# Moving a routed part ahead of the dense one, halving bursts of indirect DMAs and merging a gate product in a fused token-mixing, state-space and mixture-of-experts layer

## The reference

```
h  = prelu((dgamma * (q k^T)) v Wo + bo)        # q, k, v = x Wq + bq, ...; no softmax
n  = layernorm(h)
A  = exp(-softplus(n Wd + bd));  u = (1 - A) * (n WB + bB) * (n Wx + bx)
s_t = A_t * s_(t-1) + u_t                        # scan over 1024 tokens
h  = h + ((n WC + bC) * s) Wy + by
n  = layernorm(h)
top 2 of 16 experts of softmax(n gate_w + gate_b), their weights made to sum to 1
h  = h + sum over the 2 experts of weight * (silu(n w1) * (n w2)) w3
```

## Time and profile before

| | |
|---|---|
| median of 3 timed runs | 258.33 us (256.31 to 261.71) |
| span of the profiled execution | 331.5 us; no time of its own is given beside the span |
| mean granted TensorE clock in it | 0.846 of full speed |
| TensorE busy | 257.1 us, 78% of the span |
| VectorE, ScalarE, GpSimd busy | 160.1, 119.7, 98.2 us |

### The profile page before, as it was taken

How to read it: one execution, slowest core, us unless ns; L and a number is a source line. 1 busy time by engine, 2 the same in 40 slices (tenths; PEclk the granted TensorE clock), 3 DMA queues, 4 the chain that set the end, 5 groups by cost and what they waited for, 6 DMA issues and landing times.

```text
span 331.5 us, 4678 instructions
## 1 busy us (share of the span) xinstructions
PE 257.1 (78%) x1645; PEld 156.7 (47%) x1645; DVE 160.1 (48%) x283; ACT 119.7 (36%) x283; POOL 98.2 (30%) x119
## 2 busy tenths in 40 slices
PE   8999999988935976258829995169964899952995
PEld 7443332532411323136529884168642698621563
DVE  1453649789805993167705610053410466710664
ACT  1302561764108711467534541022320344311341
POOL 4000000004760077303771047600476000674000
PEclk9999999999985999658965997555796599995699
DMA  7999800000111101332221675995121323021101
GB/s 191 371 388 278 170 0 0 4 0 12 40 51 57 33 20 52 89 95 73 55 58 44 154 160 131 209 222 114 41 59 28 83 65 78 19 44 20 34 16 32
DMA packets 45990, 29.74 MB, mean 90 GB/s; under 512 B 32688, under 2 KB 41072, under 8 KB 45456
## 3 DMA queue, kind: packets, MB, share of 16 engines
q1 hardware_dynamic: 30416, 23.15, 27.1%
q10 hardware_dynamic: 12480, 3.15, 4.3%
q0 software_dynamic: 3072, 3.15, 3.9%
HBM read 20.46 MB, written 8.98 MB: 89 GB/s over the span
## 4 chain that ended last, share of the span: by engine, by line
PE 52%; another core or an unknown queue 19%; ACT 11%; DVE 10%; issue 7%; ACTq 0%; POOL 0%; DVEq 0%; POOLq 0%
PE ring L1013 10%; PE ring L971 9%; PE turn L988 7%; PE side L1025 5%; PE acc L816 4%; PE ring L802 4%; ACT squares L611 3%; PE side L843 3%; DVE mixed L1141 2%; PE ring L759 2%; PE side L775 2%; ACT n L629 2%; PE acc L934 1%; DVE state L1190 1%
## 5 line engine op out<-in xcount | busy, mean ns | idle before, releaser
L559 POOL DMA_INDIRECT slots<-n,slot_i x48 | 47.8, 996 | 121.9 <-DVE slot_i L1256 108.2
L1283 DVE TENSOR_TENSOR act<-ring,silu 128x512 f32<-128x512 f32 x56 | 38.4, 690 | 89.5 <-ACT silu L681 68.6
L569 POOL DMA_INDIRECT back_v<-results,slot_i x48 | 46.5, 968 | 81.4 <-DMA results<-res 67.7
L681 ACT ACTIVATE silu<-ring 128x512 f32<-128x512 f32 x56 | 33.3, 597 | 78.7 <-remote 38.5
L1141 DVE TENSOR_TENSOR mixed<-ring,dg 128x1024 f32<-128x1024 f32 x32 | 38.6, 1218 | 19.5 <-remote 10.9
L816 PE MATMUL acc<-mixed,v 128*64 128x512 f32 x128 | 34.3, 628 | 8.6 <-DVE mixed L1141 8.4
L802 PE MATMUL ring<-kq 64*128 64x512 f32 x128 | 33.5, 629 | 0.0
L1013 PE MATMUL ring<-nT,w_sb 64*128 64x256 f32 x128 | 24.2, 459 | 8.8 <-issue 8.0
L971 PE MATMUL ring<-slots_t,w_shared 64*128 64x128 f32 x192 | 19.8, 328 | 13.7 <-issue 12.7
L988 PE MATMUL turn<-w_sb,act 128*128 128x64 f32 (+1 forms) x192 | 29.1, 314 | 0.0
L988 PEld LDWEIGHTS turn<-w_sb,act 128*128 128x128 f32 x192 | 27.3, 226 | 3.0 <-issue 2.2
(11 more groups left out here) (150 smaller groups left out, 306.5 us busy)
## 6 DMA issues: line engine op xcount, KB each, us to landing
dg<-dgT SPq DMA_DIRECT2D x8, 512.0 KB, 7.8
dg<-given SPq DMA_DIRECT2D x8, 512.0 KB, 15.7
slots<-zeros SPq DMA_DIRECT2D x3, 1024.0 KB, 13.2
w_shared<-w SPq DMA_DIRECT2D x48, 64.0 KB, 2.2
slots<-slots SPq DMA_DIRECT2D x12, 256.0 KB
results<-res ACTq DMA_DIRECT2D x12, 256.0 KB, 2.9
w_sb<-w SPq DMA_DIRECT2D x2, 1024.0 KB, 14.3
xs<-xT SPq DMA_DIRECT2D x4, 256.0 KB, 6.5
```

Of the source, the lines that this page charges most:

```text
L559: pool.indirect_dma_start(out=slots_dram[r], out_offset=bass.IndirectOffsetOnAxis(ap=slot_i[:, r, k, i:i + 1], axis=0), in_=n2[:, u % 2, i ...
L569: pool.indirect_dma_start(out=back_v[:, r, i, k, :], out_offset=None, in_=results_dram[r], in_offset=bass.IndirectOffsetOnAxis(ap=slot_i[: ...
L681: s.activation(silu[:, n % 2], hidden_banks(n)[:, :, 0:PAIRS * P], ACT.Silu).then_inc(silu_done, 1)
L1283: dve.tensor_tensor(act[:, n % ACT_BUFS], hidden_banks(n)[:, :, PAIRS * P:2 * PAIRS * P], silu[:, n % 2], ALU.mult).then_inc(act_done, 1)
```

## The change

In words, in the order of the diff:

- `take_raw` now copies rows and raw gate products together (160 columns a tile); `center2` makes both in one matmul per half tile set, from the joined matrix `cg`. The logits are then read from SBUF.
- In each beat `place`, `spread` and `give_slots` come last on VectorE, and their beats are later for units 0 and 1 (slots 25 to 28) with `spread` ahead of `slots`. On ScalarE `scale_rows` comes after `relus`, `norm_squares` and `norm_std` of the next unit.
- Eight indirect DMAs are waited for before the other eight of a part are issued, in scatter and gather.
- All 32 dense groups come after r2. The spread of the dispatch matrix is cut into 8 loads instead of 4, and placed after slot loads 10 and 11; `weigh` begins at pair 10, two pairs ahead of use. Combines come earlier, result buffers are 4 instead of 2.
- The first pair of routed groups is issued at beats 62 to 68; the first turned slots go through the bank `ring`.
- At the start 30 warm-up matmuls stand instead of 70, two loads are issued from ScalarE's queue, and V1, K1, Q1 of the first half are projected at beat 2.
- The fifth set of shared weights is loaded after the fourth slot load instead of ahead of the first.

```diff
-    "center2": (16, 17), "turn_h": (21, 17), "count": (24, 21), "owner_row": (27, 14), "prelu": (0, 0),
+    "center2": (16, 17), "turn_h": (20, 19), "count": (24, 24), "owner_row": (31, 27), "prelu": (0, 0),
-    "logits": (19, 18), "mark0": (19, 19), "one0": (22, 19), "mark1": (22, 20), "one1": (22, 21), "place": (25, 24),
-    "slots": (25, 24), "spread": (25, 27), "owners": (30, 35), "weights": (24, 22), "dispatch": (4, 22),
+    "logits": (19, 18), "mark0": (19, 19), "one0": (22, 19), "mark1": (22, 20), "one1": (22, 21), "place": (27, 25),
+    "slots": (28, 25), "spread": (27, 25), "owners": (33, 30), "weights": (24, 22), "dispatch": (4, 22),
...
-WEIGHTS_AFTER = (-2, -2, -2, -2, -1, 3, 3, 6, 7, 7, 9, 11)
-
-GIVEN_AFTER = 9
-SPREAD_AFTER = 9
+WEIGHTS_AFTER = (-2, -2, -2, -2, 3, 3, 3, 6, 7, 7, 8, 8)
+
+GIVEN_AFTER = 10
+SPREAD_AFTER = {10: (0, 1), 11: (2, 3, 4, 5, 6, 7)}
+FIRST_WEIGH = 10
...
-FFN_BEAT = 65
-
-FFN_RATES = (1, 2, 1, 2, 1, 1, 0, 1, 0, 1, 1, 1, 2, 0, 1, 1, 1, 1, 2, 4, 0, 3, 0, 1)
+FFN_BEAT = 62
+
+FFN_RATES = (4, 1, 0, 0, 3, 1, 1, 0, 0, 0, 0, 0, 0, 1, 1, 2, 0, 1, 1, 1, 1, 2, 4, 0, 3, 0, 1)
-RES_BUFS = 2
-GIVEN_LOADS = 4
+RES_BUFS = 4
+GIVEN_LOADS = 8
-DENSE_RUNS = (0, 0, 8, 24)
+DENSE_RUNS = (0, 0, 0, 32)
-COMBINE_AFTER = (13, 14, 20, 22, 24, 27)
-WARM = 50
-WARM2 = 20
+COMBINE_AFTER = (11, 13, 16, 18, 22, 25)
+WARM = 30
...
                 for i in range(UT):
+                    if i == UT // 2:
+                        pool.wait_ge(scattered[r], 16 * UT)
                     for k in range(2):
...
-                s.activation(n2[:, u % 2].rearrange("p i d -> p (i d)"), side[:, 1, :], ACT.Copy).then_inc(raw_taken, 1)
+                s.activation(n2[:, u % 2].rearrange("p (k t) c -> p k t c", k=2), cg_tiles(), ACT.Copy).then_inc(raw_taken, 1)
...
-                    mm = pe.matmul(side[:, 1, t * P:(t + 1) * P], hT[:, u % 2, t * P:(t + 1) * P], center_m[:, :],
+                    mm = pe.matmul(side[:, t // 2, t % 2 * CG:(t % 2 + 1) * CG], hT[:, u % 2, t * P:(t + 1) * P], cg[:, :],
                                    start=True, stop=True)
                 mm.then_inc(cen_done[1], 1)
-                for t in range(TT):
-                    mm = pe.matmul(side[:, 0, t * 2 * NE:(t + 1) * 2 * NE], hT[:, u % 2, t * P:(t + 1) * P], gate_w[:, :],
-                                   start=True, stop=True)
-                mm.then_inc(raw_done, 1)
```

More of the change, by code:

```diff
@@ L67 @@
 VW, VB, VO, VCOLS = 0, 128, 256, 320
+CG = P + 2 * NE
 BEAT = {
@@ L143, in due @@
     units = ROUTED_UNITS if name in ROUTING else (DENSE_UNIT,) if name in DENSE_WORK else range(UNITS)
-    return [u for u in units if m - unit_end(u) == BEAT[name][u == LAST]]
+    last = ROUTED_UNITS[-1] if name in ROUTING else LAST
+    return [u for u in units if m - unit_end(u) == BEAT[name][u == last]]
 def scores_at(m):
@@ L378, in turned_sum, with cg_tiles @@
             return side[:, 1, 0:GB * D]
+        def cg_tiles():
+            return side[:, :, 0:2 * CG].rearrange("p k (t c) -> p k t c", c=CG)
         def count_bank(u):
@@ L495, in _ @@
                     store_given()
-                if n == SPREAD_AFTER:
-                    for i in range(GIVEN_LOADS):
-                        spread_given(i)
+                for i in SPREAD_AFTER.get(n, ()):
+                    spread_given(i)
                 for k in range(len(SHARED_NO)):
@@ L567, in gather @@
                 for i in range(UT):
+                    if i == UT // 2:
+                        pool.wait_ge(gathered[r * COMBINES], 16 * UT)
                     for k in range(2):
@@ L605, in norm_squares @@
                     s.wait_ge(raw_taken, u + 1)
-                rows_ = (turn[:, :], n2[:, u % 2].rearrange("p i d -> p (i d)"))[which]
                 if u == LAST:
-                    s.activation(squares[:, :, :].rearrange("p i d -> p (i d)"), rows_, ACT.Square).then_inc(squared[which], 1)
+                    rows_ = rows2(u) if which else turn[:, :].rearrange("p (t c) -> p t c", c=P)
+                    s.activation(squares[:, :, :].rearrange("p (t b) d -> p t (b d)", b=BH), rows_, ACT.Square).then_inc(squared[which], 1)
                     return
                 for i in range(UT):
-                    last = s.activation(squares[:, i, :], rows_[:, i * D:(i + 1) * D], ACT.Square, accum_out=stats[:, which, 0, i:i + 1])
+                    row_i = row2(u, i) if which else turn[:, i * D:(i + 1) * D]
+                    last = s.activation(squares[:, i, :], row_i, ACT.Square, accum_out=stats[:, which, 0, i:i + 1])
                 last.then_inc(var_done[which], 1)
@@ L736, in _ @@
                     norm_std(0, u)
+                for u in due("rows2", m):
+                    if u < LAST:
+                        scale_rows(u)
                 for u in due("tanh_table", m):
@@ L952, in hidden @@
                     pe.wait_ge(ld_w12, 32)
+                if n == 1 and q == 0:
                     pe.wait_ge(mixed_done, ALL_STEPS)
@@ L1304, in expert_piece @@
             def expert_piece(i, piece):
-                if piece in (0, 1):
-                    if 2 * i + 2 in DENSE_POS[:NE]:
-                        weigh(DENSE_POS.index(2 * i + 2) + piece)
+                if piece in (0, 1) and 0 <= 2 * (i - FIRST_WEIGH) < NE:
+                    weigh(2 * (i - FIRST_WEIGH) + piece)
                 if piece in (2, 3) and 0 <= i < ALL_PAIRS:
@@ L1349, in _ @@
                     dve.tensor_copy(gate_w[:, :], side[:, 0, 0:2 * NE]).then_inc(gate_w_done, 1)
-                for u in due("place", m):
-                    place(u)
-                for u in due("slots", m):
-                    give_slots(u)
-                for u in due("spread", m):
-                    spread(u)
                 for u in due("owners", m):
@@ L1389, in _ @@
                     residual(u)
+                for u in due("place", m):
+                    place(u)
+                for u in due("spread", m):
+                    spread(u)
+                for u in due("slots", m):
+                    give_slots(u)
                 for n, piece in expert_pieces_at(m):
```

69 lines of the change are left out of this document (38 added, 31 removed).

## The result

The changed kernel takes 262.78 us (median of 4 runs, 261.54 to 263.77) against 258.65 us of the kernel before (4 runs beside it, 256.31 to 261.71). The ratio is 1.0199, 95% interval 1.0122 to 1.0277: slower, clear of the noise. I had forecast 243.5.

The account below looks back on a forecast made before the run. It took TensorE to bound the kernel nearly everywhere, with one real stop at pair 7. Terms -3.0 - 2.5 - 1.0 + 1.0 + 2.5 - 16.0 + 4.2 = -14.8 took 258.3 to 243.5 us; range 233 to 256.5.

Parts of the forecast that it names:

- The third part behind the second: Dense groups four pairs later, `weigh` at pair 10: the whole wait at pair 7 goes, -16.0 us, bounds -12.3 and -21.5.
- the stop: Wait at pair 7 for the dispatch matrix's spread to land, priced at 21.5 us with the slow clock behind it.
- rival (a): Pair 7's wait small in timed runs, or replaced: about 255 us; 0.24 shared with (c), one slow half wait.
- Combines and gathers: VectorE's `weigh` and combines at pairs 13 and 16, plus GpSimd's gather chain ending late: +4.2 us, bounds 0 and +9.
- The start: Fewer warm-up matmuls let K0 start at 4.2 us instead of 7.47: -3.0 us, bounds 0 and 3.3.
- The merged gate product: In the mixing, L882's separate 32-column passes go, saving 0.8 us in each of three units: -2.5 us, bounds 0 and -2.9.
- the routing last: Routing steps and scaled rows no longer stand ahead of the mixing's other steps: -1.0 us, bounds +2 and -3.
- The first slots: Slots land at 114.8 us, their copy ahead of u2's `keep`, against earlier slot loads: net +1.0 us, bounds -3 and +5.
- The early pair in unit 3: Two table loads and a silu enter u3's serial chain: net +2.5 us, bounds -1 and +3.9.

Follow-up runs that it names:

- the old order: The kernel before plus only the six half waits after the eighth indirect DMA of each scatter and gather: 258.38 us, ratio 0.9992; its trace spans 256.7 us.
- the late pair: The changed kernel with the first pair of groups and first slots at their beats of before: 257.87 us, ratio 0.9956; in a later series 256.49, ratio 0.9857.
- e9_all_but_mixing: The kernel before plus new start and new order of the end, without merged gate product, late routing and early pair: 261.26 us, ratio 1.0122.
- the small spread: The late pair with each load of the spread cut to an eighth of its columns: 250.68 us, ratio 0.9654.
- e16_spread_paced: The late pair with the spread's last four loads each held until the weighing has advanced: 321.03 us in the disturbed series, 257.55 us, ratio 0.9898, when run again.
- the early pair with the small spread: The changed kernel with an eighth of the columns in each load of the spread: 329.65 us in the disturbed series, not run again.

## Why the prediction was wrong, point by point

**The third part behind the second (-16.0, bounds -12.3 and -21.5): the step that failed.** I took the price of the stop from the profile: first landing 13.2 us after the issue, 13.6 us of waiting, 8.4 of slow clock. In the old order, undisturbed, the same loads land in

```profile
DMA to landing us min/median/max: 6.0/12.7/19.6
```

and TensorE waits 7.8 us, with 1.65 of slow clock in the first product behind: 9.5 to win, below my lower bound. The bound of 12.3 was no measurement: it was the rest of a subtraction (258.3 less 246.0) whose parts came from an execution 73 us longer. I had written rival (a) with just this argument and gave it a small share. Of the 19.5 us between the forecast change (-14.8) and the difference of the spans (+4.7), 10.8 are in this term and the next.

**Combines and gathers (+4.2, bounds 0 and +9): right in kind, wrong in what is late.** I counted VectorE at pairs 13 and 16 and GpSimd's own chain, and asked of the spread only whether it reaches its reader in time. It does: the first `weigh` starts at 190.54 without idle time. But its loads run beside a slot load (6.06 us to landing) and results stores (median 5.4, in one trace up to 18.0), and ScalarE's issue of one store took 3.18. I kept 2.9 for every landing. That the bytes cost 5.3 to 5.8 us was tested with the late pair only. VectorE slows GpSimd a little: a gather that meets a `weigh` takes 1.17 to 1.39 us in the late pair's traces in place of 0.94. The mean of all is 989 ns, against 968 and 981 in the old order, so the price is 0.4 to 1.0 us (48 x 0.008 and 48 x 0.021). I had set the Trainium skill's factor of five against it, and misread its scope: the same page ("SBUF — State Buffer", Who interferes with whom) says that `tensor_tensor`, which `weigh` is, has no two-port mode, and that with two inputs in SBUF it contends with GpSimd's reads alone. The trace agrees in that no gather takes several times as long; the factor of five never bore on this change. The two terms together came to -1.0 (110.25 to 109.28), where the sum had -11.8; with the late pair they are -2.5 and -3.0 in its two traces (107.8 and 107.23 against 110.25).

**The start (-3.0): right.** -2.7 at the first ReLU; in e9_all_but_mixing the fourth ReLU was at 114.6 against 117.4, so nothing takes it back. It isn't in every execution: with the same start the first ReLU came at 34.2 to 35.4 us in the undisturbed traces but one, and at 37.15 in that of the small spread.

**The merged gate product (-2.5) and the routing last (-1.0): too large.** The work goes: L882 and L886 held TensorE 4.6 + 3.9 us, L900 5.6. But `give_slots` now lies between the scan and `tnh`, so TensorE waits before the output product (7.0 us in all with the late pair, 3.0 in the old order). At the fourth ReLU the late pair is at 114.36, and the kernel without these two parts at 114.6: 0.2 us. Unit 3's chain is 0.8 shorter (28.31 against 29.07). So -1.0 for -3.5, and not even that for sure: in the late pair's other trace the fourth ReLU is at 115.79 and the chain takes 29.24.

**The first slots (+1.0, bounds -3 and +5): the size was off, and the mechanism named in half a sentence.** I had "ScalarE's copy of these slots stands ahead of u2's `keep`, with the scan behind it", and priced it by when the slots land (114.8; measured 110.1). The copy waits for the transposes, and these for their place in TensorE's queue, whenever the slots land: +5.2 (3.7 by the late pair's other trace).

**The early pair in unit 3 (+2.5, bounds -1 and +3.9): right.** +3.0 (2.1 by the other trace), the two table loads and the SiLU in the chain, as I had them: putting them back gave 2.4.

Sum of the measured terms: -2.7 - 1.0 + 5.2 + 3.0 - 1.0 = +3.5 us. With 1.2 more (first to third ReLU 53.01 against 51.84 with the late pair: products at half clock in unit 1, behind a wait of 2.28 us that both have) it is 4.7, the difference of the spans. All of these are differences of single traces, with the late pair's fastest as the link. So the result lay outside my range for three reasons: the largest term was priced in a disturbed execution, its successor was not looked for among the transfers, and the first slots cost 3.7 to 5.2 us in place of 1.0.

## What to carry to other kernels

When a profiled execution is far longer than the timed ones, get a trace whose span fits the times (a variant that changes nothing will do) before a wait of it is priced. When a large transfer is moved off a stop, list every store and load that it will then run beside, and who waits for each; here its bytes cost 5.3 to 5.8 us, most of it, by the traces, behind one slot load. And an instruction that is moved early on an in-order engine must be asked what it waits for there on the *other* engine's queue, not only when its data arrive; here a copy of 0.6 us stood 7 us and held `keep`, a scan and a whole unit behind it (3.7 to 5.2 us of the kernel).

## What the runs showed of the hardware that I had not expected

One kernel on one chip has two very different times. The kernel before took 258.4 to 261.1 us (medians) in six series and 330.59 us (11 runs, 328.94 to 333.11) in one, on the same chip number (14) as the first experiments, where it took 260.08. The profile of before (331.5) is of the same kind. The mark of these disturbed executions is the chain's share without a releaser, 19% before; in the trace of e16_spread_paced it is

```profile
PE 52%; DVE 15%; issue 12%; ACT 10%; another core or an unknown queue 9%; POOL 0%; DVEq 0%; ACTq 0%; POOLq 0%
```

and the stretches lie where GpSimd issues indirect DMAs, as in this window of 10 us (PE busy, and the clock fell to 0.50):

```profile
200.00:210.00 10.00, 6.41 (x32) 4.43 (x31) 0.69 (x1) 1.79 (x3) 7.18 (x8) 0.50 0.31 71
```

TensorE then goes in steps: products of 0.2 to 0.5 us, apart by 0.3 to 1 us, with no wait named. The late pair with the paced spread, which has the half waits, was 2.9% below the kernel before there by the medians (321.03 against 330.59, no interval), but the early pair with the small spread, which has them too, only 0.3% (329.65). Whether the half waits help there was not tried, and what brings these executions on is open too.

The granted clock also differs between executions of one kernel at equal waits. In the two traces of the late pair, the output product of unit 2 waits 3.22 us both times and then takes 1.08 us in one and 1.98 in the other; the fourth ReLU stands at 114.36 and 115.79. That alone can set two runs of one kernel a microsecond or more apart.
